# Expert routing by fixed regions of 2048 rows, chosen and scattered inside the output projection, with layer 1 modulation and clearing in the attention

## What is computed

```python
mod = (_silu(L1_c) @ L1_wmod).reshape(4, 6, 1, 512)   # sa, ca, ga, sb, cb, gb
ga = (2 * (ga >= 0) - 1) * jnp.maximum(jnp.abs(ga), 0.25)   # gb alike
# layer 0: 8 heads, 6 experts a head, gated attention, then Wo
x = x + ga * attention(h)
h = _layernorm(x) * (1 + cb) + sb
# routed FFN, 8 experts, top 2 of the router's logits
_, choices = jax.lax.approx_max_k(logits32, k=2)
xs_order = choices.ravel().argsort()
sorted_xs = x_flat[xs_indices, :]          # 4096 rows, grouped by expert
gate_out = ragged_dot(sorted_xs, w_gate, group_sizes=tokens_per_expert)
activation = gelu(gate_out[:, 0, :]) * gate_out[:, 1, :]
out = combine(ragged_dot(activation, linear, tokens_per_expert), weights)
```

## Time and profile before

| what | value |
|---|---|
| median of 3 runs | 2815.18 us (2814.02 to 2816.53) |
| the profiled execution | 2821.85 us, its span 2820.1 us |
| attention, first scores to last gated row | 385 to 1068 us |
| output projection, first product to the end | 1083 to 1221 us |
| start of the expert stage to its first gate product | 1221.2 to 1295.6 us |
| the 23 expert blocks | 1296 to 1722 us |

### The profile page before, as it was taken

One profiled execution on the slowest core, in us unless ns is written; L12 is line 12 of the kernel. 1 busy time (PEld: TensorE's weight loads), 2 busy tenths in 40 slices (PEclk: granted clock), 3 DMA queues, 4 the chain that ended last, 5 costly groups with the idle time before them and its releaser, 6 DMA issues. The chain is left out here.

```text
span 2820.1 us, 34326 instructions
## 1 busy us (share of the span) xinstructions
PE 2440.6 (87%) x10156; PEld 1660.9 (59%) x10156; DVE 1751.6 (62%) x2565; ACT 1275.8 (45%) x2546; POOL 1083.1 (38%) x1090
## 2 busy tenths in 40 slices
PE   7999959999999986966999994769898757699889
PEld 5778825555555544845888883535445216588767
DVE  4330239999999994644555553679999977211133
ACT  3223038999999982324555552732323113211121
POOL 0102035666666654542000002278898973111110
PEclk9999979999999997967999997889999988899989
DMA  5253343434444427757766765544444435100022
GB/s 176 84 170 129 97 107 106 128 107 124 112 119 117 113 61 226 252 194 256 233 227 227 233 209 160 172 151 153 161 166 156 176 118 173 53 23 22 19 93 67
DMA packets 269652, 399.91 MB, mean 142 GB/s; under 512 B 33392, under 2 KB 116352, under 8 KB 269536
## 3 DMA queue, kind: packets, MB, share of 16 engines
q1 hardware_dynamic: 234848, 347.64, 39.0%
q10 hardware_dynamic: 28704, 33.08, 3.4%
q0 software_dynamic: 5984, 17.73, 1.9%
HBM read 304.09 MB, written 94.31 MB: 141 GB/s over the span
## 5 line engine op out<-in xcount | busy, mean ns | idle before, releaser
L1020 ACT ACTIVATE attn_probs<-attn_ps_score,attn_nmax 128x512 f32<-128x512 f32 x512 | 342.8, 674 | 2.6 <-DVE attn_nmax L1094 2.6
L2480 PE MATMUL scan_ps_o<-scan_qs,scan_sel 128*128 128x512 f32 x512 | 265.3, 635 | 84.3 <-DVE scan_qs L2424 81.7
L2442 DVE TENSOR_TENSOR_SCAN scan_st<-scan_ps_dec,scan_kv 128x512 f32<-128x512 f32 x256 | 305.4, 1207 | 9.9 <-POOL scan_kv L2394 9.8
L928 PE MATMUL attn_ps_score<-attn_KK,attn_X 64*128 64x512 f32 x512 | 215.0, 466 | 20.6 <-ACT attn_probs L1020 20.2
L2480 PEld LDWEIGHTS scan_ps_o<-scan_qs,scan_sel 128*128 128x128 f32 x512 | 88.9, 194 | 232.2 <-DVE scan_qs L2424 153.9
L1108 DVE SCALAR_TENSOR_TENSOR attn_mixed<-attn_probs,attn_cf,attn_mixed 128x512 f32<-128x512 f32 x256 | 193.5, 756 | 9.1
L1083 DVE TENSOR_REDUCE attn_raw<-attn_ps_score 128x2 f32<-128x1024 f32 x128 | 156.4, 1222 | 42.4 <-PE attn_ps_score L928 41.1
L928 PE MATMUL attn_ps_score<-attn_KL,attn_X 64*128 64x512 f32 x512 | 172.9, 422 | 0.0
L85 POOL MEMSET head_ident<- 128x128 f32 x1 | 0.2, 204 | 439.6 <-POOLq L2828 439.6
L2394 POOL TENSOR_TENSOR scan_kv<-scan_vb,gla_gk 128x512 f32<-128x512 f32 x128 | 160.7, 1277 | 12.2 <-DMA scan_vb<-gv 5.4
L928 PE MATMUL attn_ps_score<-attn_KK,attn_Y 64*128 64x512 f32 x512 | 160.1, 397 | 1.3 <-POOL attn_Y L822 1.3
(11 more groups left out here) (438 smaller groups left out, 6803.8 us busy)
## 6 DMA issues: line engine op xcount, KB each, us to landing
scan_vb<-gv SPq DMA_DIRECT2D x256, 256.0 KB
moe_raw<-in_L_ffn_gating SPq DMA_DIRECT2D x92, 512.0 KB
attn_spread<-rows SPq DMA_DIRECT2D x64, 384.0 KB
moe_raw<-in_L_ffn_linear SPq DMA_DIRECT2D x46, 512.0 KB, 5.4
rows_x<-out_zeros SPq DMA_DIRECT2D x23, 512.0 KB, 8.4
moe_xb<-rows_x SPq DMA_DIRECT2D x23, 512.0 KB, 6.1
rows_y<-moe_y ACTq DMA_DIRECT2D x23, 512.0 KB, 6.5
sg<-proj_tile SPq DMA_DIRECT2D x32, 256.0 KB, 2.0
```

The lines of the kernel that those rows point to most:

```text
L928: last = nc.tensor.matmul(ps_score[n][:, j, :], weights, y[p][half, :], start=(r == 0), stop=(r == len(terms) - 1))
L1020: nc.scalar.activation(probs[b][:, at_j, :], ps_score[n][:, j, :], ACT.Exp, bias=nmax[b][:, at_j:at_j + 1], accum_out=Z[b][:, at_j:at_j + ...
L2442: V.tensor_tensor_scan(st[r][:, :], ps_dec[n % 2][:, :], kv[r][:, :], 0.0, ALU.mult, ALU.add).then_inc(st_ready, 1)
L2480: nc.tensor.matmul(ps_o[w][:, :], sel[:, P - GPH - GPH * d:2 * P - GPH - GPH * d], qs[i % RING][:, :], start=(d == 0), stop=(d == HALF - 1 ...
```

## The change

Five edits:

1. `rows_x` becomes 8 regions of 2048 rows, one for each expert, 16384 rows in all. A token's row is the region's start plus a running count (`base`), so that it can be written before the counts of all tokens are known.
2. Ranking, counting and row numbers are done a sequence at a time in project_out (`choice`, `count`, `places`), and POOL scatters from there: tile n-10 beside tile n, four more tiles in the stage's tail, the last four at the start of the expert stage. Logits move from behind tile 3 to behind tile 2.
3. The expert stage makes the tables of blocks, with a start row for each block; the first block's expert is always 0, and its weights are asked for at once.
4. Layer 1's modulation is made in the attention: `mod_w` loaded on SP in units 0, 1 and 28, six groups of four products on PE after tiles of units 0 and 28 to 31, lifted and stored by ACT. Its two gates are finished by POOL in the expert stage, and its first two sixths are read back by SP in 8 small transfers.
5. `rows_x` is cleared in the attention, 512 rows (1 MB) behind every unit's inputs, 32 transfers, 33.5 MB in place of 11.8 MB.

The diff, cut to what the steps below speak of:

```diff
@@ attention
+        fill = s["rows_x"].rearrange("(u p t) d -> u p t d", u=U, p=P)
+        MOD_LOADS = {0: (0, 1), 1: (2, 3), U - 4: (4, 5)}
+        MOD_AT = {(0, 3): 0, (U - 4, 2): 1, (U - 3, 2): 2, (U - 2, 2): 3, (U - 1, 1): 4, (U - 1, 2): 5}
+        LIFT_AT = {(1, 0): 0, (U - 4, 3): 1, (U - 3, 3): 2, (U - 2, 3): 3, (U - 1, 2): 4, (U - 1, 3): 5}
+        mod_bank = [ps_o, ps_exp[SHARED], ps_exp[SHARED], ps_exp[SHARED], ps_exp[AB], ps_exp[SHARED]]
...
+                for k in listed(MOD_LOADS, u) or ():
+                    wmod = a["L1_wmod"].rearrange("(c p) m -> p c m", p=P)
+                    sp.dma_start(mod_w[k][:, :, :], wmod[:, :, k * D:(k + 1) * D]).then_inc(mod_in[k], 16)
+                sp.dma_start(at(fill, u).rearrange("o p t d -> p (o t) d"),
+                             zeros[:, :].unsqueeze(1).to_broadcast([P, E * B * T // (U * P), D])).then_inc(zeroed, 16)
...
+            def modulation(u, t):
+                k = listed(MOD_AT, u, t)
+                if k is None:
+                    return
+                pe.wait_ge(mod_in[k], 16)
+                if k:
+                    n = (min(u + 1, U - 1)) * 2 + EXPANDED[AB if mod_bank[k] is ps_exp[AB] else SHARED]
+                    pe.wait_ge(qh_ready, n)
+                    pe.wait_ge(whole_ready, n)
+                if k == 5:
+                    pe.wait_ge(mod_taken, 4)
+                for c in range(DC):
+                    last = nc.tensor.matmul(mod_bank[k][0:B, :], s["sT"][:, 1, c, :], mod_w[k][:, c, :], start=(c == 0),
+                                            stop=(c == DC - 1))
+                last.then_inc(mod_done, 1)
...
+                act.wait_ge(mod_done, k + 1)
+                if k >= 2:
+                    act.wait_ge(mod_stored[k % 2], 16 * (k // 2))
+                nc.scalar.activation(mod_row[k % 2], mod_bank[k][0:B, :], ACT.Copy, bias=1.0 if k in (1, 4) else 0.0
+                                     ).then_inc(mod_taken, 1)
+                act.wait_ge(mod_taken, k + 1)
+                act.dma_start(s["mod"][1, :, k * D:(k + 1) * D], mod_row[k % 2]).then_inc(mod_stored[k % 2], 16)
...
@@ project_out
+            def scatter(n):
+                pool.wait_ge(rows_ready, n // TT + 1)
+                pool.wait_ge(shifted, n + 1)
+                scatter_rows(nc, s, n)
...
+                    if n % TT == 1 and n > TT:
+                        scale(n // TT - 1)
+                    if n >= SCATTER_BEHIND:
+                        scatter(n - SCATTER_BEHIND)
             if h is not None:
+                for n in range(NT - SCATTER_BEHIND, NT - 2 * TT):
+                    scatter(n)
                 scale(B - 1)
+                for n in range(NT - 2 * TT, NT - TT):
+                    scatter(n)
...
+            def count(b):
+                if b == 0:
+                    pe.wait_ge(route_const, N_ROUTE)
+                pe.wait_ge(chosen_ready, b + 1)
+                flat = s["chosen"][:, TT * b:TT * (b + 1), :].rearrange("p n e -> p (n e)")
+                for k, x in enumerate((earlier, ones)):
+                    last = nc.tensor.matmul(ps_logit[:, (1 + k) * TT * E:(2 + k) * TT * E], x[:, :], flat, start=True, stop=True)
+                last.then_inc(count_done, 1)
...
-                if h is not None and n % TT == TT - 1 and n > TT:
+                if h is not None and n % TT == 2 and n > TT:
                     logits(n // TT - 1)
+                if h is not None and n % TT == 0 and n >= 2 * TT:
+                    count(n // TT - 2)
             turn(B - 1)
             if h is not None:
+                count(B - 2)
                 logits(B - 1)
+                count(B - 1)
...
+                rc.step(V.tensor_tensor(beats[:, :, :, :], pj, pi, ALU.is_gt))
+                rc.link(V.tensor_tensor(ties[:, :, :, :], pj, pi, ALU.is_equal))
+                rc.link(V.tensor_tensor(ties[:, :, :, :], ties[:, :, :, :], below[:, :, :, :], ALU.mult))
+                rc.link(V.tensor_tensor(beats[:, :, :, :], beats[:, :, :, :], ties[:, :, :, :], ALU.add))
+                rc.link(V.tensor_reduce(rank[:, :, :], beats[:, :, :, :], AX.X, ALU.add))
+                V.tensor_scalar(s["chosen"][:, tiles, :], rank[:, :, :], 2.0, None, ALU.is_lt).then_inc(chosen_ready, 1)
+                rc.step(V.tensor_scalar(s["first_e"][:, tiles, :], rank[:, :, :], 0.0, None, ALU.is_equal))
+                rc.link(V.tensor_scalar(s["second_e"][:, tiles, :], rank[:, :, :], 1.0, None, ALU.is_equal))
...
+                dve.wait_ge(count_done, b + 1)
+                for t in range(TT):
+                    n = TT * b + t
+                    rc.link(V.tensor_tensor(base[:, n + 1, :], base[:, n, :], counts(1)[:, t, :], ALU.add))
+                V.tensor_tensor(place[:, :, :], base[:, tiles, :], counts(0), ALU.add).then_inc(placed, 1)
+                dve.wait_ge(placed, b + 1)
+                for c, one in enumerate((s["first_e"], s["second_e"])):
+                    rc.link(V.tensor_tensor(pick[:, :, :], place[:, :, :], one[:, tiles, :], ALU.mult))
+                    rc.link(V.tensor_reduce(s["row"][:, c, tiles], pick[:, :, :], AX.X, ALU.add))
+                V.tensor_copy(row_x[:, :, tiles], s["row"][:, :, tiles]).then_inc(rows_ready, 1)
...
+                    if h is not None and b:
+                        choice(b - 1)
                 if t == 2 and b:
                     after(b - 1)
+                if h is not None and t == 1 and b >= 2:
+                    places(b - 2)
+            if h is not None:
+                places(B - 2)
             after(B - 1)
+            if h is not None:
+                choice(B - 1)
+                places(B - 1)
...
@@ expert_mixture, SP and POOL
-            for k in range(6):
-                sp.dma_start(mod_w[k][:, :, :], wmod[:, :, k * D:(k + 1) * D]).then_inc(mod_in[k], 16)
-            sp.wait_ge(experts_ready, 1)
-            sp.wait_ge(mod_done, 6)
             def load_weights(n):
-                e = nc.sync.value_load(expert_of[0:1, n:n + 1], min_val=0, max_val=E - 1)
+                e = nc.sync.value_load(expert_of[0:1, n:n + 1], min_val=0, max_val=E - 1) if n else 0
...
             load_rows(0)
+            sp.wait_ge(experts_ready, 2)
...
+            for n in range(NT - TT, NT):
+                scatter_rows(nc, s, n)
...
-            pool.wait_ge(rows_ready, 1)
-            for n in range(NT):
-                for k in two:
-                    nc.gpsimd.indirect_dma_start(s["rows_x"], bass.IndirectOffsetOnAxis(row_i[:, k, n:n + 1], 0), h[:, n, :],
-                                                 None).then_inc(scattered, 16)
...
```

More of the change, by code:

```diff
@@ L682, in attention @@
         o = [m.sb(f"o{p}", [P, T]) for p in two]
+        mod_w = [m.sb(f"mod_w{k}", [P, DC, D]) for k in range(6)]
+        mod_row = [m.sb(f"mod_row{p}", [P, D])[0:B, :] for p in two]
+        zeros = m.sb("zeros", [P, D])
         ps_score = [m.ps(f"ps_score{i}", (P, 2, T)) for i in two]
@@ L719, in first_unit, with listed @@
             return isinstance(u, int) and u == 0
+        def listed(table, u, *tile):
+            return table.get((u, *tile) if tile else u) if isinstance(u, int) else None
         def left(u):
@@ L1071, in _ @@
             lift(U - 1, False)
+            for p in two:
+                act.wait_ge(mod_stored[p], 48)
         @block.vector
@@ L1178, in project_out @@
             rows = [m.sb(f"rows{p}", [P, 2, D]) for p in two]
-        if cleared is not None:
-            zeros = m.sb("zeros", [P, 2 * D])
-            zeros_ready, zeroed = m.sem("zeros_ready"), m.sem("zeroed")
+            earlier, ones = m.sb("earlier", [P, P]), m.sb("ones", [P, P])
+            beats, ties, below = (m.sb(n, [P, TT, E, E]) for n in ("beats", "ties", "below"))
+            rank, place, pick = (m.sb(n, [P, TT, E]) for n in ("rank", "place", "pick"))
+            row_x = m.sb("row_x", [P, 2, NT], I32)
+            s["row_x"] = row_x
+            route_const, route_step, chosen_ready, count_done, placed, rows_ready, scattered = (m.sem(n) for n in (
+                "route_const", "route_step", "chosen_ready", "count_done", "placed", "rows_ready", "scattered"))
+            s["scattered"] = scattered
+            N_ROUTE = 5 + E
         bank = [m.ps(f"bank{i}") for i in range(BANKS)]
@@ L1381, in _ @@
                     take(b - 1)
+                if h is not None and b and t == TT - 1:
+                    router(b - 1)
                 if h is not None and b >= 2 and t == 1:
-                    router(b - 2)
                     squares(b - 2)
@@ L1497, in expert_mixture @@
         xT = [[m.sb(f"xT_{part}{i}", [P, DC, P], F32R) for part in ("hi", "lo")] for i in range(XRING)]
-        with ExitStack() as first:
-            z = Scope(nc, first, "route", s["sems"])
-            mod_w = [z.sb(f"mod_w{k}", [P, DC, D]) for k in range(6)]
-            beats, ties, below = (z.sb(n, [P, NT, E, E]) for n in ("beats", "ties", "below"))
         W = (weights(m, 0), W1)
@@ L1586, in _ @@
```

(14 more changed lines are left out.)

244 lines of the change are left out of this document (113 added, 131 removed).

## The result

| | before | after |
|---|---|---|
| median | 2815.86 us (4 runs) | 2840.62 us (4 runs) |
| ratio, 95% interval | | 1.009 (1.0067 to 1.0113) |
| span of the profiled execution | 2820.1 us | 2838.9 us |

The account below looks back on a forecast made before the run. PE, busy 87% of the span, was taken to bound the kernel. Expert start -53, attention +73 and output projection +20 us sum to +40: 2855 us, range 2802 to 2888.

Parts of the forecast that it names:

- The start of the expert stage: Stage start to first gate product: 21.4 us against 74.4, -53 us (-55 to -47); both paths 20 us.
- The clearing in the loop: Attention units: each clearing adds 2.7 us on two full DMA engines, whose work becomes 22.6 us a unit.
- Their free time per unit: Attention: idle time of the two DMA engines carrying queries and keys, between 0.6 and 1.1 us, taken as 0.6.
- Rival A: Attention: clearing transfers hide, attention costs only 25 us, whole 2807 us; decided below 0.6 us a unit; chance 0.20.
- Rival B: Attention: clearing holds SP in every unit, which grows by 3.5 us; whole 2893 us; chance 0.12.
- Unit 0: Attention, behind unit 0: four modulation products wait for `mod_w0`, so PE resumes 16.6 us late.
- The late groups: Units 28 to 31: two product groups hide, three cost up to 1.7 us each plus a 0.6 lift: +5.
- the expected backlog: Attention: late transfers on two DMA engines add 68 us, hiding the product groups in units 28 and 29.
- The output projection: Whole stage, through PE waits, clock, POOL work and tail: +20 us, between +8 and +28.
- The waits in front of `count`: Output projection, tiles 8 and 12: PE stands 5.7 us each for the ranking, 11 us for both.
- The tail: End of output projection: later logits, then ranking, count and places in series after the last sequence: +4 us.
- The sum: Whole kernel: -53 + 73 + 20 = +40 us, giving 2855 us; forecast's chance 0.68.

Follow-up runs that it names:

- experiment 2: Changed kernel clearing 2 MB a unit in place of 1, the second into a spare table: 2902.5 us, ratio 1.0306.
- experiment 12: Changed kernel clearing 3 MB a unit, two of them into spare tables, query and key loads as they are: 2977.5 us, ratio 1.0566.
- Experiment 4: Changed kernel with the first two groups of modulation products moved behind tiles 2 and 3 of unit 28: 2840.4 us, ratio 1.0083.
- Experiment 5: Kernel of experiment 2 with queries and keys each loaded by two transfers of 64 partitions, over sixteen engines: 2804.7 us, ratio 0.9965.
- experiment 6: Changed kernel with counting products, row numbers and scatters one tile later in the output projection: 2832.5 us, ratio 1.0065.
- experiment 7: Changed kernel with POOL scaling a sequence's rows only once DVE has ranked the sequence before: 2834.3 us, ratio 1.0079.
- Experiment 3: Changed kernel with modulation groups 1 to 5 making only one of their four products: 2827.9 us, ratio 1.0053.
- experiment 1: Kernel before plus clearing 1 MB of a spare table behind each unit's inputs: 2813.4 us, ratio 0.9997.
- experiment 9: Kernel before with queries and keys each loaded by two transfers of 64 partitions: 2800.5 us, ratio 0.9952.
- experiment 8: Changed kernel, 1 MB clearing, with queries and keys each loaded by two transfers of 64 partitions: 2805.6 us, ratio 0.9962.

## Why the prediction was right in sign and off in its largest term

**The start of the expert stage: right.** -53 forecast, -50.8 measured. The rows landed 5.5 us behind the last scatter and not 1.8; the forecast had both paths at 20 us and no price for their meeting.

**The clearing in the loop: mechanism right, point of onset wrong.** The failed step is "Their free time per unit is between 0.6 us [...] and 1.1 us". I had read it from the DMA share: 0.13 is two engines busy. But a busy engine need not move bytes at its full rate. A stretch of the kernel before, in the middle of what I called full:

```profile
731.00:734.00 3.00, 2.83 (x17) 1.68 (x15) 2.93 (x6) 3.00 (x8) 1.30 (x3) 1.00 0.14 32
```

The share is the same 0.14 and the rate 32 GB/s, where other such stretches have 49. By bytes, with the rate of experiments 2 and 12, the sum is: 262 KB of queries and keys and 116 KB of the rest are 378 KB, 17.0 us at 22.2 GB/s. That leaves 3.5 us of 20.5, not 0.6. A clearing costs 65.5 KB, 3.0 us. It fits once (20.0 us), not twice (22.9; measured 23.1), and three times make 25.9 (measured 25.6). The last two agree by making, since the rate comes from them. But a rate was to be had before: 364 GB/s for sixteen engines is 22.8 for one, and 116 GB/s over 20.5 us gives the bytes. With it the three are 19.5, 22.3 and 25.2 us, within 0.8 of what came. The first stood in the prediction, for another purpose, and the second in its rows. What keeps the two engines at 32 GB/s for 3 us I did not settle.

Rival A therefore named the right outcome for the loop ("the transfers hide"), but its point of decision ("a clearing price below 0.6 us a unit") compared the right price with the same wrong free time. Rival B (SP held) was seen and did no harm: in the stretch from 716 to 745 us single issues took SP up to 4.41 us, and POOL's waits for what came late were 0.8 us at most.

**Unit 0: right, a little small.** 16.6 forecast, 19.6 measured. Experiment 4 shows more than I had seen: without the group the same backlog stops PE at units 2 and 3. Experiment 5 shows the cause, the same two engines.

**The late groups: the step that was mis-sized.** "the other three cost up to 1.7 us each on PE (four products took 1.88 with the last one's tail)" misread its row. The x4 there counts instructions, and `values` makes two products at that place, so the row says 0.9 us a product and some 3.6 for four. The products themselves also had a row in the kernel before, 7.03 us for two groups. A group is eight instructions, 3.6 us, and they stand where PE has hardly any idle time (before, it was 91 to 97% busy from 984 to 1045 us); nothing of the expected backlog was there to hide two of them. +16.7 in place of +5 in this trace, and some 13.5 in those of experiments 6 and 7, where the stretch took 116.5 us. Experiment 3 confirms the cause by 12.9 us reckoned and 12.7 measured for three quarters.

**The output projection: +30 in place of +20, outside the 8 to 28 I gave.** The waits in front of `count` were 7.0 us each, not 5.7, since DVE's ranking ran beside POOL's work. The rest is clock and the counting products themselves: over the tiles the granted clock was 0.86, against 0.90 before. The tail cost 7.0 in place of 4: logits start 13.4 us after the last product instead of 11.1, and ranking, counting and row numbers behind them take 8.3 us to the stage's end instead of 3.5.

**The sum.** +40 was forecast and +25 came by the medians. It came out near because the loop was 48 us too dear, and three terms were too cheap by 3, 12 and 10 us; the sign was carried by the terms that I had held to be small. That the time fell into the range was luck: one error of 48 us was met by three of the other sign.

## What to carry to other kernels

Free time of a DMA engine is read from bytes and its full rate, not from its busy share; a transfer costs nothing until the fullest engine's bytes by that rate reach the period, and from there its whole price. Before adding transfers, look for one that uses few engines: spreading it was worth 15 us in the kernel before and 35 in the changed one, where the whole change had cost 25. Price a matrix product from a row of that very product, and check how many products the row's count of instructions stands for. Put work for PE where PE waits, not where it is merely off another engine's path.

## What the runs showed of the hardware

- An operation on DVE can wait out one on POOL. The third operation of the ranking takes 0.42 us alone; started 0.6 us into POOL's `out_o_lo` of 2.79 us it took 2.46 and ended 0.3 us after it. This agrees with the Trainium skill (SBUF — State Buffer, section "SBUF: two separate sides"): the two engines share one pair of ports, and whichever instruction starts first keeps it to its end. The operation just ahead, with both inputs from `logit` read broadcast, started 0.15 us into the same POOL operation and took 0.42 us; by the page's words on two inputs from SBUF one of the two should have waited for the other. DVE's did not. POOL's took 2.78 to 2.83 us each time it met the ranking so, and at most 2.50 otherwise, so it may be the one that was held; starts on POOL are too rough in the profile to tell.
- The same code can differ by 7 us in one stage. The products of the output projection took 116.3 us in the trace of before and 109.3 in that of experiment 1, which has the same stage (114.8 in experiment 9); the granted clock over them was 0.90 and 0.96:

```profile
1083.00:1200.00 117.00, 111.02 (x499) 92.06 (x499) 67.28 (x110) 35.33 (x55) 53.78 (x28) 0.90 0.79 265
...
1087.00:1196.00 109.00, 104.27 (x494) 86.68 (x495) 69.06 (x110) 35.36 (x55) 53.50 (x27) 0.96 0.85 284
```

  The first row is of the kernel before, the second of experiment 1. What decides it I did not find; a difference of a few us in one trace of that stage is therefore no result by itself. The changed stage, as the changed kernel and experiments 2, 3, 4, 5, 8 and 12 have it, took 139.4 to 139.6 us in each of its seven traces, so against the traces of before it costs 23 to 30 us more.
